# A sum of two scan tiles, moved from GpSimd and VectorE to an accumulating DMA

## The reference

```python
def step(h, inps):
    u_t, dt, B_t, C_t = inps
    dA = jnp.exp(dt[:, :, None] * A)
    h = dA * h + (dt * u_t)[:, :, None] * B_t[:, None, :]
    y = jnp.einsum('bdn,bn->bd', h, C_t) + Dv * u_t
    return (h, y)
...
yh = jnp.transpose(y1 + y2 + y3 + y4, (0, 2, 3, 1))
```

## Time and profile before

| what | value |
|---|---|
| median of 3 runs | 18655.86 us (18643.19 to 18657.38) |
| span of the profiled execution, from its first to its last instruction | 18660.7 us |
| the profiled execution's own time | the profile gives the span alone, 4.8 us above the median |
| busy share of the span, PE, PEld, DVE, ACT, POOL | 90%, 55%, 86%, 81%, 67% |
| `l1_scans`, first scan's start to last scan's end | 9030.2 to 16217.4 us |
| DMA moved over the span | 170 GB/s on average |

### The profile page before, as it was taken

How to read it: one execution, slowest core, us unless ns; L and a number is a source line. 1 busy time by engine, 2 the same in 40 slices (tenths; PEclk the granted TensorE clock), 3 DMA queues, 4 the chain that set the end, 5 groups by cost and what they waited for, 6 DMA issues and landing times. The chain is left out here.

```text
span 18660.7 us, 271066 instructions
## 1 busy us (share of the span) xinstructions
PE 16820.2 (90%) x78344; PEld 10186.0 (55%) x78344; DVE 16050.6 (86%) x12158; ACT 15162.6 (81%) x24326; POOL 12567.1 (67%) x6247
## 2 busy tenths in 40 slices
PE   8799998899996798879899999999999999989798
PEld 3355554455552364455566666666666666547374
DVE  3799998899996486479899999999999999879698
ACT  7699996799992555557899999999999999845556
POOL 0099993599990474135799999999999999700101
PEclk9899998899997899999999999999999999999899
DMA  5788886788879677777433333333333333441313
GB/s 175 230 242 245 236 250 208 233 246 237 247 223 249 217 224 222 253 237 277 166 113 112 113 112 119 113 112 113 112 112 114 122 113 113 125 138 54 104 53 101
DMA packets 898273, 3166.02 MB, mean 170 GB/s; under 512 B 145638, under 2 KB 180170, under 8 KB 872140
## 3 DMA queue, kind: packets, MB, share of 16 engines
q1 hardware_dynamic: 817612, 3011.91, 51.1%
q10 hardware_dynamic: 79104, 136.10, 2.4%
HBM read 2342.21 MB, written 805.32 MB: 169 GB/s over the span
## 5 line engine op out<-in xcount | busy, mean ns | idle before, releaser
L1788 DVE TENSOR_TENSOR_SCAN l1s_h<-l1s_da,l1s_pd 128x1024 f32<-128x1024 f32 x3072 | 6778.1, 2268 | 241.5 <-PE l1s_pd L1720 163.4
L1831 ACT ACTIVATE l1s_dm<-l1s_dut,l1s_bt 128x384 f32<-128x384 f32 x7424 | 4056.8, 604 | 74.0 <-PE l1s_pd L1720 73.8
L1814 ACT ACTIVATE l1s_da<-l1s_dl,l1s_a 128x1024 f32<-128x1024 f32 x3072 | 3496.9, 1138 | 32.0 <-DVE l1s_h L1788 31.0
L1720 PE MATMUL l1s_pd<-l1s_id,l1s_dm 128*128 128x128 f32 x22272 | 2967.8, 274 | 36.4 <-DVE l1s_h L1788 33.9
L1720 PEld LDWEIGHTS l1s_pd<-l1s_id,l1s_dm 128*128 128x128 f32 x22272 | 2561.9, 142 | 487.7 <-issue 287.9
L1694 POOL TENSOR_TENSOR l1s_pb<-l1s_h,l1s_cc 128x1024 f32<-128x1024 f32 x1024 | 2517.8, 2459 | 95.0 <-DVE l1s_h L1788 83.4
L1698 POOL TENSOR_TENSOR l1s_pa<-l1s_sm,l1s_cc 128x1024 f32<-128x1024 f32 x1024 | 2433.1, 2376 | 0.0
L1731 PE MATMUL l1s_py<-l1s_pb,l1s_both 128*128 128x512 f32 x4096 | 2157.4, 609 | 197.1 <-POOL l1s_pb L1694 197.1
L1689 POOL TENSOR_TENSOR l1s_sm<-l1s_h 128x1024 f32<-128x1024 f32 x928 | 2203.5, 2374 | 122.8 <-DVE l1s_h L1788 122.6
L1731 PE MATMUL l1s_py<-l1s_pa,l1s_id 128*128 128x512 f32 x4096 | 2113.4, 598 | 0.3 <-POOL l1s_pa L1698 0.3
L2654 POOL TENSOR_TENSOR l0sf_pr<-l0sf_h,l0sf_cc 128x1024 f32<-128x1024 f32 x768 | 1813.8, 2380 | 71.1 <-DVE l0sf_h L2736 54.8
(11 more groups left out here) (318 smaller groups left out, 30375.1 us busy)
## 6 DMA issues: line engine op xcount, KB each, us to landing
l1s_cc<-crows SPq DMA_DIRECT2D x1024, 512.0 KB, 3.7
l0sf_cc<-l0crowsf SPq DMA_DIRECT2D x512, 512.0 KB, 5.5
l0sb_cc<-l0crowsb SPq DMA_DIRECT2D x512, 512.0 KB, 5.5
l0sf_cc<-l0crowsf SPq DMA_DIRECT2D x512, 256.0 KB, 7.1
l0sb_cc<-l0crowsb SPq DMA_DIRECT2D x512, 256.0 KB, 7.1
dls<-l1p_dl SPq DMA_DIRECT2D x192, 512.0 KB, 7.0
duts<-l1p_dut SPq DMA_DIRECT2D x64, 1536.0 KB, 5.9
l1s_dut<-duts SPq DMA_DIRECT2D x64, 1536.0 KB, 7.2
```

Source lines behind the costliest of these rows:

```text
L1720: mm = pe.transpose(pd[:, s % 2, blk * 128:blk * 128 + 128], dm[:, rnd % 2, blk, j * 128:j * 128 + 128], idt[:, :])
L1788: dve.tensor_tensor_scan(h[:, s % 4, :], da[:, j, :], pd[:, s % 2, :], 0.0, ALU.mult, ALU.add)\
L1814: act.activation(da[:, j, :], dl[:, half, j, :], ACT.Exp, scale=a[:, HT * half + j, n:n + 1])\
L1831: ins = act.activation(dm[:, rnd % 2, blk, :], dut[:, half, blk, :], ACT.Identity, scale=bt[:, half, blk, n:n + 1])
```

## The change

The ring `h` grows from four tiles to six, and `sm` goes. In every round POOL waits for the second scan and issues a transfer from tile 1's slot of `h` into tile 0's slot that adds to what lies there. After `pb` it waits for this transfer to land, and multiplies tile 0's slot by `cc` into `pa`. DVE makes no sums. The first scan of a round now waits for `pa` of two rounds before, the third for `pb` of two rounds before, the second for neither. Two semaphores for the transfers come from outside of the stage and are handed down through `build`.

```diff
-    SUMS_ON_DVE = (6, 13, 25)
+    RING = 6
...
-        da = r.sb("da", [128, 3, HW]); h = r.sb("h", [128, 4, HW])
-        sm = r.sb("sm", [128, 2, HW]); pa, pb = (r.sb(n, [128, 2, HW]) for n in ("pa", "pb"))
+        da = r.sb("da", [128, 3, HW]); h = r.sb("h", [128, RING, HW])
+        pa, pb = (r.sb(n, [128, 2, HW]) for n in ("pa", "pb"))
...
-                        if rnd not in SUMS_ON_DVE:
-                            pool.wait_ge(scan, nth(s + 1))
-                            pool.wait_ge(proda, nth(q - 2))
-                            pool.tensor_tensor(sm[:, rnd % 2, :], h[:, rnd * HT % 4, :], h[:, (rnd * HT + 1) % 4, :], ALU.add)\
-                                .then_inc(summed, 1)
+                        low, other, high = (h[:, (rnd * HT + t) % RING, :] for t in range(HT))
+                        pool.wait_ge(scan, nth(s + 1))
+                        pool.sem_inc(begun, 1)
+                        pool.dma_start(low, other, accum_op=ALU.add).then_inc(s_sum[rnd % 2], 16)
                         pool.wait_ge(scan, nth(s + 2))
                         pool.wait_ge(s_cc[rnd % 4], b * (ROUNDS // 4 * 16) + rnd // 4 * 16 + 16)
                         pool.wait_ge(yb, nth(q - 2))
...
+                        pool.tensor_tensor(pb[:, rnd % 2, :], high, cc[:, rnd % 4, :], ALU.mult).then_inc(prodb, 1)
+                        pool.wait_ge(s_sum[rnd % 2], b * (ROUNDS // 2 * 16) + rnd // 2 * 16 + 16)
                         pool.wait_ge(ya, nth(q - 2))
...
+                        pool.tensor_tensor(pa[:, rnd % 2, :], low, cc[:, rnd % 4, :], ALU.mult).then_inc(proda, 1)
...
                         if j == 0:
+                            dve.wait_ge(proda, nth(b * ROUNDS + rnd - 2))
+                        if j == 2:
                             dve.wait_ge(prodb, nth(b * ROUNDS + rnd - 2))
-                        else:
-                            dve.wait_ge(summed, nth(b * ROUNDS + rnd - 1))
...
-                        if rnd in SUMS_ON_DVE and j == 2:
-                            dve.wait_ge(scan, nth(b * STEPS + s - 1))
-                            dve.wait_ge(proda, nth(b * ROUNDS + rnd - 2))
-                            dve.tensor_tensor(sm[:, rnd % 2, :], h[:, rnd * HT % 4, :], h[:, (rnd * HT + 1) % 4, :], ALU.add)\
-                               .then_inc(summed, 1)
```

More of the change, by code:

```diff
@@ L1580, in _, with l1_scans @@
                 turns(act, turn, 1, 1)
-def l1_scans(nc, dls, u1, duts, bts, crows, ys, alog, skip, ident, pairs):
+def l1_scans(nc, dls, u1, duts, bts, crows, ys, alog, skip, ident, pairs, s_sum):
     T, HT = 6, 3
@@ L1612, in l1_scans @@
         s_y = [r.dma_sem(f"y{s}") for s in range(2)]
-        aexp, anegd, skipd, multlo, multhi, diagd, expd, trd, scan, summed, prodb, proda, yb, ya, finb, fina, passed = r.step_sems(
-            "aexp", "aneg", "skipd", "multlo", "multhi", "diagd", "expd", "trd", "scan", "summed", "prodb", "proda", "yb", "ya", "finb", "fina", "passed")
+        r.taken += s_sum
+        aexp, anegd, skipd, multlo, multhi, diagd, expd, trd, scan, begun, prodb, proda, yb, ya, finb, fina, passed = r.step_sems(
+            "aexp", "aneg", "skipd", "multlo", "multhi", "diagd", "expd", "trd", "scan", "begun", "prodb", "proda", "yb", "ya", "finb", "fina", "passed")
         consts = [(a[:, :, :], alog), (dd[:, :, :], skip), (idt[:, :], ident), (both[:, :], pairs)]
@@ L1693, in body @@
                         pool.wait_ge(yb, nth(q - 2))
-                        pool.tensor_tensor(pb[:, rnd % 2, :], h[:, (rnd * HT + 2) % 4, :], cc[:, rnd % 4, :], ALU.mult)\
-                            .then_inc(prodb, 1)
-                        pool.wait_ge(summed, nth(q))
+                        pool.tensor_tensor(pb[:, rnd % 2, :], high, cc[:, rnd % 4, :], ALU.mult).then_inc(prodb, 1)
+                        pool.wait_ge(s_sum[rnd % 2], b * (ROUNDS // 2 * 16) + rnd // 2 * 16 + 16)
                         pool.wait_ge(ya, nth(q - 2))
-                        pool.tensor_tensor(pa[:, rnd % 2, :], sm[:, rnd % 2, :], cc[:, rnd % 4, :], ALU.mult)\
-                            .then_inc(proda, 1)
+                        pool.tensor_tensor(pa[:, rnd % 2, :], low, cc[:, rnd % 4, :], ALU.mult).then_inc(proda, 1)
                 with pool.Fori(0, IMAGES) as b:
@@ L1784, in body @@
                         if j == 0:
+                            dve.wait_ge(proda, nth(b * ROUNDS + rnd - 2))
+                        if j == 2:
                             dve.wait_ge(prodb, nth(b * ROUNDS + rnd - 2))
-                        else:
-                            dve.wait_ge(summed, nth(b * ROUNDS + rnd - 1))
-                        dve.tensor_tensor_scan(h[:, s % 4, :], da[:, j, :], pd[:, s % 2, :], 0.0, ALU.mult, ALU.add)\
+                        dve.tensor_tensor_scan(h[:, s % RING, :], da[:, j, :], pd[:, s % 2, :], 0.0, ALU.mult, ALU.add)\
                            .then_inc(scan, 1)
-                        if rnd in SUMS_ON_DVE and j == 2:
-                            dve.wait_ge(scan, nth(b * STEPS + s - 1))
-                            dve.wait_ge(proda, nth(b * ROUNDS + rnd - 2))
-                            dve.tensor_tensor(sm[:, rnd % 2, :], h[:, rnd * HT % 4, :], h[:, (rnd * HT + 1) % 4, :], ALU.add)\
-                               .then_inc(summed, 1)
                         if rnd == 0 and j == 2 and not first:
@@ L2820, in ahead, with build @@
     return c, s, c * SEQS + s
-def build(nc, x, w, out):
+def build(nc, x, w, out, s_sum):
     def dram(name, shape, dt=F32):
@@ L2889, in build @@
     l1_scan_inputs(nc, u1, ws, dls1, duts, bts, crows, w["ident"])
-    l1_scans(nc, dls1, u1, duts, bts, crows, ys1, ws["alog"], ws["skip"], w["ident"], w["pairs"])
+    l1_scans(nc, dls1, u1, duts, bts, crows, ys1, ws["alog"], ws["skip"], w["ident"], w["pairs"], s_sum)
     l1_out_proj(nc, x0, ys1, z1, ws, x1)
@@ L3052 @@
     out = nc.dram_tensor("out", (IMAGES, C, HW), F32, kind="ExternalOutput").ap()
-    build(nc, aps.pop("x"), aps, out)
+    with nc.semaphore("sums0") as even, nc.semaphore("sums1") as odd:
+        build(nc, aps.pop("x"), aps, out, [even, odd])
     r = run_bass_kernel_spmd(nc, [{f"in_{name}": a for name, a in arrays.items()}], core_ids=[0])
```

## The result

The changed kernel takes 21,851.7 us (median of 4 runs, 21,836.8 to 21,861.2) against 18,649.5 us: slower, ratio 1.1715 with a 95% interval of 1.1699 to 1.1731. The loss is 3202 us where 1671 were forecast. It all lies in the stage of the change: from the first scan to the end of the last it went from 7187 to 10,397 us, and the whole span grew by 3198. A round takes 10,397 / 1024 = 10.15 us, not 7.02.

The account below looks back on a forecast made before the run. POOL and ACT were taken to bound the stage together. A round of 6.3 + 2.35 = 8.65 us over 1024 rounds adds 1671 us to 18,656, giving 20,330 us; range 18,540 to 22,270.

Parts of the forecast that it names:

- POOL has a chain of its own: POOL's queue: issue of the transfer, its landing, `pa`, next issue; this alone sets the pace, 8.65 us a round.
- P: Shortest round POOL's queue allows: L plus 2.35 us for `pa`, forecast 8.65 us.
- L: Time from POOL's issue of the transfer to its landing: between 5.45 and 7.2 us, hidden below 4.56.
- the middle, 6.3: Value taken for L in us, between transfer landing first (5.45) and last (7.2) beside the `cc` load.
- the bracket: Bounds on L on the DMA queues: 5.45 us if the transfer lands first, 7.2 if last.
- the sign of sharing: In the changed profile, the `cc` load itself should land later than 3.7 us.
- The split under L: Transfer's landing: 1.95 us fixed plus two reads of 1.75, 5.45 alone; with the `cc` load up to 7.2.
- The estimate from the other page of the Trainium skill: POOL's transfers: 2.0 us plus bytes at 436 GB/s, so 3.2 us for 512 KB, 4.4 for 1024 KB.
- the likeliest case: Transfer lands after 5.45 to 7.2 us, POOL's queue sets the pace: 19,450 to 21,250 us, chance 0.48.
- rival (d): POOL must prepare the transfer itself, or the add runs below copy rate: 22,270 us at L 8.2; chance 0.22.
- The first rival: At POOL's wait before `pa`: transfer lands within 4.56 us, ACT sets the pace: 18,544 to 18,580 us; chance 0.18.
- The sign that every engine's busy time would be as before: In the stage's changed profile, busy times unchanged except POOL's 2203 us and DVE's 115 us.

Follow-up runs that it names:

- e1: Changed kernel without the transfer and the wait for it, so tile 1 is never added: 18,639 us.
- e6: Changed kernel with POOL's order altered: transfer, `pb`, then `pa` of the round before; ring of nine tiles: 18,941 us, ratio 1.0162.
- e11: Changed kernel with the `dut` and `dl` loads cut to 32 columns after the first image: 21,651 us.
- e9: Changed kernel with one wait moved: SP's `cc` load is released by `pb`, some 3 us after the transfer starts: 19,392 us.
- e8: As e10, but POOL also makes one of ACT's eight scaled blocks of a round: 18,651 us, ratio 1.0005.
- e10: As e6, but POOL's `pa` of the round before stands ahead of the third scan's wait and `pb`: 18,657 us, ratio 1.0007.
- e2: Changed kernel with the transfer as a plain copy from POOL, nothing added: 19,987 us.

## Why the prediction was right, and what it mis-sized

- **The mechanism was right.** "POOL has a chain of its own": issue, landing, `pa`, issue. P = L + 2.28 holds in the changed kernel, e1 shows that the transfer and the wait for it are the whole loss, and e6 removes 91% of it by the order on POOL, with the landing as long as in the changed kernel.
- **The size of L was off.** The step that failed reads "I take the middle, 6.3, because the two queues share the same engines and neither has a head start". The median is 7.3 and the average up to `pa` 7.87: the transfer lands after its `cc` load in 992 rounds of 1024, the upper end of the bracket. The load itself lands after 4.5 and not 3.7, which the prediction had as the sign of sharing. Of the 1531 us by which the loss was under-forecast, (7.3 - 6.3) x 1024 = 1024 are this; (7.87 - 7.3) x 1024 = 584 are mostly rounds in which something else stood in the way: the image's loads 200 (e11), and for the rest the instruction packets are suspected, 283 rounds at 1.4 us more being about 390; and from the start of `pa` to the next issue it is 2.28 and not 2.35, 72 the other way.
- **The split under L was off too.** Alone the transfer takes 4.6 us (e9), not 5.45, and the neighbour costs 2.7, not at most 1.75. That the bracket's upper end, 7.2, is so near the median of 7.3 is luck: the two errors cancel. The estimate from the other page of the Trainium skill, "DMA: Bandwidth & Descriptors" in "Anatomy of one DMA — SWDGE (gpsimd) path", 4.4 us for 1024 KB, was near the 4.6 alone, and I set it aside because SP's loads lay above it. That estimate leaves out the neighbour, which decided here.
- **The range held by its width.** The time lies above the likeliest case's 19,450 to 21,250, in the band that rival (d) had up to 22,270, but neither of (d)'s reasons makes it up: the transfer alone lands sooner than forecast, POOL's preparation included, and its engine time is 2.06 times the plain copy's, no more than the forecast had counted. The range itself reached from a gain to a loss of 3616 us, so that it held says little.
- **The first rival's price was wrong.** A hidden transfer was to bring 76 to 112 us by ACT's pace. e1 brings 17 within the spread of the kernel before, and e8 and e10 none within their intervals. The 112 us were ACT's idle time, and 105 of them end with PE's transposes and the scans, not with POOL; the chance of 0.18 for faster should have gone to no change.
- **What was hidden stayed hidden.** `pb` (now 2.65 us beside the issue) and POOL's 0.87 us of issue lie inside L, and PE at a granted clock of 0.89 inside the round: 7787 / 1024 = 7.60 of 10.15 us. The sign that every engine's busy time would be as before did not hold for PE, which took 991 us more, nor for ACT, 189 more.

## What to carry to other kernels

A transfer that takes the place of an engine's instruction should not be waited for, in the same round, in the queue that issues the next one: with a round between issue and wait, 91% of the loss (e6) or all of it (e10) was gone. Ask what the wait's release starts elsewhere; here one product released both the load and the transfer, and moving one wait by 3 us was worth 2460 us. And before paying for less work on an engine, leave the work out once: that run shows what there is to gain, here nothing clear of the spread.

## What the runs showed that was not expected

- Of two transfers that start together the accumulating one is delayed by more than the other's engine time: 2.7 us, where that of the `cc` load is about 1.5 by the estimate from the earlier trace rows. The load is delayed by 0.8. A load of 16 KB beside it cost 1.0 us.
- POOL's product beside the preparation of an accumulating transfer takes 2.65 us and not 2.37; behind the plain copy of e2, whose issue takes 0.59 us and not 0.87, it stays at 2.37.
- A transfer with one 16 KB packet of instruction loading beside it landed 1.4 us later on average, over 283 of them; seen in time, not tested.
